# A right-hand side solved by two 64-row blocks instead of a last inversion level, 128-row operands for 8-row matmuls, and new turn strings

## The reference

```
S = S * exp(g_t)
u = (v_t - k_t . S) * b_t
S = S + outer(k_t, u)
o_t = q_t . S
```

## Time and profile before

| | before |
|---|---|
| median of three runs | 3089.29 us |
| the profiled execution | 3073.01 us |
| its span, first to last instruction | 3071.2 us |
| TensorE matmul busy | 2502.6 us (81%) |
| VectorE busy | 2245.6 us (73%) |
| ScalarE busy | 1247.8 us (41%) |
| GpSimd busy | 641.2 us (21%) |
| mean granted TensorE clock | 0.906 of full speed |

### The profile page before, as it was taken

How to read it: one execution, slowest core, us unless ns; L and a number is a source line. 1 busy time by engine, 2 the same in 40 slices (tenths; PEclk the granted TensorE clock), 3 DMA queues, 4 the chain that set the end, 5 groups by cost and what they waited for, 6 DMA issues and landing times.

```text
span 3071.2 us, 61542 instructions
## 1 busy us (share of the span) xinstructions
PE 2502.6 (81%) x22808; PEld 2004.1 (65%) x22808; DVE 2245.6 (73%) x5056; ACT 1247.8 (41%) x2761; POOL 641.2 (21%) x528
## 2 busy tenths in 40 slices
PE   2477978879887887978889797887988788897897
PEld 1166766757766576766757676575766657676686
DVE  1668777787877778787687877778787777877762
ACT  0233533435344253533425353243534424353342
POOL 0222122131212222122131212313121122202210
PEclk9869989989899898989989998998989989898998
DMA  4000000000000000000000000000000000000000
GB/s 119 2 2 3 2 8 3 7 3 7 2 3 8 2 7 3 6 2 3 7 3 7 2 3 8 3 7 3 7 2 3 7 3 7 3 4 5 1 5 2
DMA packets 24718, 21.52 MB, mean 7 GB/s; under 512 B 7210, under 2 KB 21443, under 8 KB 24403
## 3 DMA queue, kind: packets, MB, share of 16 engines
q1 hardware_dynamic: 24402, 17.14, 2.0%
HBM read 15.00 MB, written 2.13 MB: 6 GB/s over the span
## 4 chain that ended last, share of the span: by engine, by line
PE 60%; DVE 18%; issue 13%; POOL 4%; ACT 3%; SPq 1%; DMA 1%; DVEq 0%; POOLq 0%; ACTq 0%
PE banks L984 8%; PE banks L1160 8%; PE banks L1150 8%; PE banks L1034 6%; PE banks L918 4%; PE banks L927 3%; DVE wide L1332 3%; PE banks L976 3%; DVE wide L1344 2%; PE banks L855 2%; PE banks L962 2%; PE banks L1019 2%; PE banks L1026 2%; PE banks L897 2%; POOL lg L536 2%
## 5 line engine op out<-in xcount | busy, mean ns | idle before, releaser
L532 POOL TENSOR_TENSOR wide<-wide 128x512 f32<-128x512 f32 x128 | 243.5, 1902 | 872.5 <-DVE wide L1352 560.7
L1461 DVE SCALAR_TENSOR_TENSOR wide<-pad,conv,wide 128x256 f32<-128x256 f32 x864 | 389.1, 518 | 0.0
L984 PE MATMUL banks<-inv,mats 64*64 64x64 f32 x5120 | 198.0, 237 | 141.8 <-DVE inv L1505 104.6
L1344 DVE TENSOR_TENSOR_SCAN wide<-wide 128x1024 f32<-128x1024 f32 x128 | 308.4, 2409 | 1.9 <-ACT wide L634 0.3
L634 ACT ACTIVATE wide<-small,a_neg 128x255 f32<-128x255 f32 x512 | 217.8, 497 | 201.8 <-DVE wide L1344 198.9
L984 PEld LDWEIGHTS banks<-inv,mats 64*64 64x64 f32 x5120 | 185.2, 152 | 160.1 <-issue 159.2
L1150 PE MATMUL banks<-inv,up 128*128 128x256 f32 x1024 | 264.9, 387 | 0.0
L1160 PE MATMUL banks<-down,inv 128*128 128x128 f32 x2048 | 257.7, 277 | 0.0
L768 ACT ACTIVATE inv<-banks,up1b 128x256 f32<-128x256 f32 x512 | 215.0, 481 | 105.0 <-PE banks L1150 104.8
L1160 PEld LDWEIGHTS banks<-down,inv 128*128 128x128 f32 x2048 | 249.9, 192 | 5.8
L984 PE MATMUL banks<-inv 64*64 64x64 f32 x5120 | 189.0, 233 | 29.0 <-DVE inv L1513 28.9
(11 more groups left out here) (281 smaller groups left out, 5160.1 us busy)
## 6 DMA issues: line engine op xcount, KB each, us to landing
gates_bc<-gate_rows SPq DMA_DIRECT2D x32, 128.0 KB, 2.9
up<-in_W SPq DMA_DIRECT2D x1, 2048.0 KB
x<-in_x SPq DMA_DIRECT2D x16, 128.0 KB, 2.1
out<-xn_y SPq DMA_DIRECT2D x16, 128.0 KB, 1.9
wide<-in_wmod SPq DMA_DIRECT2D x2, 384.0 KB
con<-in_con SPq DMA_DIRECT2D x1, 724.0 KB
w_k<-in_Wk SPq DMA_DIRECT2D x1, 512.0 KB
w_q<-in_Wq SPq DMA_DIRECT2D x1, 512.0 KB
```

Source lines behind the costliest of these rows:

```text
L532: g.tensor_tensor(ypart[p % 2], r[:, 0:512], r[:, 512:1024], ALU.add).then_inc(a_yp.h, 1)
L984: last = t.matmul(PS[a:b, out, h * HALF:(h + 1) * HALF], weights(h, a, b), values(h, a, b), start=True, stop=True)
L1344: v.tensor_tensor_scan(state[st % 2], decay[st % 2], drive[st % 2], 0.0, ALU.mult, ALU.add).then_inc(a_h.h, 1)
L1461: v.scalar_tensor_tensor(dst, src, w, dst, ALU.mult, ALU.add).then_inc(c_conv.h, 1)
```

## The change

The last level is dropped: LEVELS ends at 32. What it made is replaced by a solve in two blocks per chunk. c_top multiplies the upper 64 rows of R by the inverse of the upper block, ScalarE copies the result to top_x; c_low multiplies it by the off-diagonal block of M, and VectorE adds that to the lower half of R; c_X multiplies this by the inverse of the lower block. All are 64x64 weights with 32 columns, 8 heads each. TTf is gone. keep_warm now stands ahead of c_top of chunk 1, and of c_low and c_X of both chunks.

cfT, rank_sb and w_dt get 128 rows, zero below the eighth or ninth, and the products L883 and L826 read all 128. The product with down0b in b_out still reads nine rows.

```diff
-LEVELS = [2, 4, 8, 16, 32, 64]
+LEVELS = [2, 4, 8, 16, 32]
...
-APPLY = [("c_R", 0), ("c_X", 0), ("c_U", 0), ("c_O", 0), ("c_S",), ("c_o", 0), ("c_kS",), ("c_R", 1), ("c_X", 1),
+APPLY = [("c_R", 0), ("c_top", 0), ("c_low", 0), ("c_X", 0), ("c_U", 0), ("c_O", 0), ("c_S",), ("c_o", 0), ("c_kS",), ("c_R", 1), ("c_top", 1), ("c_low", 1), ("c_X", 1),
...
-        "yyyyyyyyyxyxyyyyyyxyyxyyyyyyyyyyyxyyyyxxyyyxxyxxyxxyxxyxxyyxxxxxxxxyyxxyyxxyxxxxyxxyyyyxyxxyxyyx"
-        "yxyyyyyyyyyyyxyyxyyxyyxyyxyyxyyxyyyyyxxxxxxxxxxxxxxxxx"),
+        "yyyyxxyyyyyyyxyxyyyxyyxxyxyxyyyxxyyxxyxxyxyxyyyxxxxxxxxyyxxyyyxxxxxxyxxyyyyxyxyxyyyyxyxxyyyyyyyy"
+        "xyyxyxyxyyxyyyyyxxyyxxyxxxxxxxxyyxxxxxxyyx"),
-        "yyyyyyxyxyyyxyyxyxyyxyxyyyyxyyyyxxxyyxyxxyxxxyxxxyxyxxyxyxxxxxyxxxyyxxyxxyxxyxxyxxxxyxyyxyxxxyxy"
-        "xyxxyxxyxxyxyxyyxxxxxxxxx"),
+        "yyyxyyyyxyxyyyxyyxyyxxyyyxyxxxyxyyyxxyxyxxxyxxyxyxyxyxxxyxxxyxxxyyxxyxyxxxyxxyxxxxyxyyxyxxxxyxyy"
+        "xxxxxyxxyxxxxxxyxyxxyxy"),
-        "yyyyyxyyxyyyyxxyyyyxyxyyyxyyyxyxyyxxxyxxxyxxyyxxyxxxxyyxyyyxxxyxyyyyxyyxyxyxyxyxyxyxyyxxxxxxxxxx"),
+        "yxyxyyxyyxxyxxyyxxyyyxxxyyxyxxxxyyxxxyxxyxyxyyyxxxyyxyxyyyxyxyxxyxyxyyxyxxxxxyyxxxxx"),
-        "xxxxxxxxxyxyxxyxxxxxxxxxxxx"),
+        "xxxxxxxxyxxxyxyxxxxxxxxxxxx"),
...
-        w_dt = sb("w_dt", [RANK, CB * P])
+        w_dt = sb("w_dt", [P, CB * P])
...
-        rank_sb = sb("rank_sb", [RANK, T])
+        rank_sb = sb("rank_sb", [P, T])
...
-        cfT = sb("cfT", [9, T])
+        cfT = sb("cfT", [P, T])
...
-        TTf = sb("TTf", [P, TILES, NH, P])
+        top_x = inv[0:HALF, 6, 256:512].rearrange("p (h v) -> p h v", v=DV)
...
-            g.memset(TTf[:], 0.0)
+            g.memset(cfT[:], 0.0)
+            g.memset(rank_sb[:], 0.0)
...
-            def lev_T(i, l, ch):
-
-                if l + 1 == NL:
-                    s.wait_ge(c_Tp.h, c_Tp.at(i, ch + 1))
-                    s.copy(TN[ch][0:HALF].rearrange("p h t -> p (h t)"), PS[0:HALF, 5 + ch, :]).then_inc(c_Tl.h, 1)
-
             def lev_TT(i, l, ch):
-                if l + 2 < NL:
+                if l + 1 < NL:
                     s.wait_ge(c_T.h, c_T.at(i, (l + 1) * TILES + ch + 1))
                 else:
                     s.wait_ge(c_TTp.h, c_TTp.at(i, l * TILES + ch + 1))
-                if l + 2 < NL:
-                    last = s.copy(TTd[ch].rearrange("p h t -> p (h t)"), bank(5 + ch))
-                elif l + 2 == NL:
-                    for a, b in HALVES:
-                        last = s.copy(TTf[a:b, ch, :, a:b], PS[a:b, 5 + ch, :].rearrange("p (h t) -> p h t", t=HALF))
-                else:
-                    last = s.copy(TTf[0:HALF, ch, :, HALF:P], PS[0:HALF, 5 + ch, :].rearrange("p (h t) -> p h t", t=HALF))
-                last.then_inc(c_TT.h, 1)
+                s.copy(TTd[ch].rearrange("p h t -> p (h t)"), bank(5 + ch)).then_inc(c_TT.h, 1)
+
+            def c_top(i, ch):
+                s.wait_ge(c_tp.h, c_tp.at(i, ch + 1))
+                s.copy(top_x.rearrange("p h v -> p (h v)"), PS[0:HALF, 3 + ch, 0:256]).then_inc(c_tx.h, 1)
...
-                    t.matmul(bank(1, T), con[0:E0, C_SEL + m * P:C_SEL + (m + 1) * P], cfT[0:E0, :], start=True,
+                    t.matmul(bank(1, T), con[:, C_SEL + m * P:C_SEL + (m + 1) * P], cfT[:], start=True,
...
-            def lev_T(i, l, ch):
-                if l + 1 == NL:
-                    t.wait_ge(c_TT.h, c_TT.at(i, (l - 1) * TILES + ch + 1))
-                    t.sem_inc(released, 1)
-                    for h in range(NH):
-                        last = t.matmul(PS[0:HALF, 5 + ch, h * HALF:(h + 1) * HALF], TTf[0:HALF, ch, h, 0:HALF], ident[0:HALF, 0:HALF],
-                                        start=True, stop=True)
-                    last.then_inc(c_Tp.h, 1)
-
             def lev_Z(i, l, ch):
-                if l + 1 < NL:
-                    t.wait_ge(c_T.h, c_T.at(i, l * TILES + ch + 1))
-                else:
-                    t.wait_ge(c_Tl.h, c_Tl.at(i, ch + 1))
+                t.wait_ge(c_T.h, c_T.at(i, l * TILES + ch + 1))
                 t.sem_inc(released, 1)
-                if l + 1 < NL:
-                    last = halves(3 + ch, lambda h, a, b: MTc[ch][a:b, h, a:b], lambda h, a, b: TN[ch][a:b, h, :])
-                else:
-                    for h in range(NH):
-                        last = t.matmul(PS[HALF:P, 3 + ch, h * HALF:(h + 1) * HALF], MTc[ch][0:HALF, h, HALF:P], TN[ch][0:HALF, h, :],
-                                        start=True, stop=True)
-                last.then_inc(c_Z.h, 1)
+                halves(3 + ch, lambda h, a, b: MTc[ch][a:b, h, a:b], lambda h, a, b: TN[ch][a:b, h, :]).then_inc(c_Z.h, 1)
 
             def lev_TT(i, l, ch):
                 t.wait_ge(c_W.h, c_W.at(i, l * TILES + ch + 1))
                 if l >= 1:
                     t.wait_ge(c_TT.h, c_TT.at(i, (l - 1) * TILES + ch + 1))
                 t.sem_inc(released, 1)
-                if l + 2 < NL or l + 2 == NL:
-                    last = halves(5 + ch, lambda h, a, b: WW[ch][a:b, h, :], lambda h, a, b: TTd[ch][a:b, h, :])
-                else:
-                    for h in range(NH):
-                        last = t.matmul(PS[0:HALF, 5 + ch, h * HALF:(h + 1) * HALF], WW[ch][HALF:P, h, :], TTf[HALF:P, ch, h, HALF:P],
-                                        start=True, stop=True)
-                last.then_inc(c_TTp.h, 1)
+                halves(5 + ch, lambda h, a, b: WW[ch][a:b, h, :], lambda h, a, b: TTd[ch][a:b, h, :]).then_inc(c_TTp.h, 1)
...
-            def c_X_(i, ch):
+            def c_top(i, ch):
                 if ch == 1:
                     keep_warm(4)
                 if ch == 0:
                     t.wait_ge(c_R0.h, c_R0.at(i, 1))
-                    t.wait_ge(c_TT.h, c_TT.at(i, NL * TILES))
+                    t.wait_ge(c_TT.h, c_TT.at(i, (NL - 1) * TILES + 1))
                 else:
                     t.wait_ge(c_R1.h, c_R1.at(i, 3))
-                per_head(3 + ch, lambda h: TTf[:, ch, h, :], R).then_inc(c_X.h, 1)
+                    t.wait_ge(c_TT.h, c_TT.at(i, NL * TILES))
+                t.sem_inc(released, 1)
+                for h in range(NH):
+                    last = t.matmul(PS[0:HALF, 3 + ch, h * DV:(h + 1) * DV], TTd[ch][0:HALF, h, :], R[0:HALF, h, :], start=True, stop=True)
+                last.then_inc(c_tp.h, 1)
+
+            def c_low_(i, ch):
+                keep_warm(7 - ch)
+                t.wait_ge(c_tx.h, c_tx.at(i, ch + 1))
+                t.sem_inc(released, 1)
+                for h in range(NH):
+                    last = t.matmul(PS[HALF:P, 3 + ch, 256 + h * DV:256 + (h + 1) * DV], MTc[ch][0:HALF, h, HALF:P], top_x[:, h, :],
+                                    start=True, stop=True)
+                last.then_inc(c_lp.h, 1)
+
+            def c_X_(i, ch):
+                keep_warm(7 - ch)
+                t.wait_ge(c_low.h, c_low.at(i, ch + 1))
+                t.sem_inc(released, 1)
+                for h in range(NH):
+                    last = t.matmul(PS[HALF:P, 3 + ch, h * DV:(h + 1) * DV], TTd[ch][HALF:P, h, :], R[HALF:P, h, :], start=True, stop=True)
+                last.then_inc(c_X.h, 1)
...
-                elif l + 1 < NL:
+                else:
                     v.wait_ge(c_TTp.h, c_TTp.at(i, (l - 1) * TILES + ch + 1))
                     v.transpose(TN[ch].rearrange("p h t -> p (h t)"), bank(5 + ch)).then_inc(c_T.h, 1)
 
             def lev_Z(i, l, ch):
                 v.wait_ge(c_Z.h, c_Z.at(i, l * TILES + ch + 1))
-                if l + 1 < NL:
-                    v.tensor_tensor(WW[ch], bank(3 + ch).rearrange("p (h t) -> p h t", t=HALF),
-                                    con[:, C_MERGE + l * HALF:C_MERGE + (l + 1) * HALF].unsqueeze(1).broadcast_to([P, NH, HALF]),
-                                    ALU.mult).then_inc(c_W.h, 1)
-                else:
-                    v.tensor_copy(WW[ch][HALF:P].rearrange("p h t -> p (h t)"), PS[HALF:P, 3 + ch, :]).then_inc(c_W.h, 1)
+                v.tensor_tensor(WW[ch], bank(3 + ch).rearrange("p (h t) -> p h t", t=HALF),
+                                con[:, C_MERGE + l * HALF:C_MERGE + (l + 1) * HALF].unsqueeze(1).broadcast_to([P, NH, HALF]),
+                                ALU.mult).then_inc(c_W.h, 1)
...
+
+            def c_low_(i, ch):
+                v.wait_ge(c_lp.h, c_lp.at(i, ch + 1))
+                if ch == 0:
+                    v.wait_ge(c_R0.h, c_R0.at(i, 1))
+                else:
+                    v.wait_ge(c_R1.h, c_R1.at(i, 3))
+                v.tensor_tensor(R[HALF:P], R[HALF:P], PS[HALF:P, 3 + ch, 256:512].rearrange("p (h v) -> p h v", v=DV),
+                                ALU.add).then_inc(c_low.h, 1)
```

22 lines of the change are left out of this document (12 added, 10 removed).

## The result

The changed kernel takes 3093.51 us (median of 20 runs, 3088.31 to 3098.63) and the kernel before 3083.76 us (20 runs, 3077.88 to 3091.03), ratio 1.0029, 95% interval 1.0021 to 1.0036: 10 us slower, where I forecast 8 us faster. The profiled executions have spans of 3086.5 and 3071.2 us, 15.3 apart.

What follows compares the result with a forecast made beforehand. No engine bounds the whole: latency limits the first stage, VectorE the scan, TensorE the projections. Terms sum to -0.35 us an iteration, times 15 -5, and -2.7 once: -8 us, 3081 us, range 3040 to 3122.

Steps and rivals of the forecast that it cites:

- the turn of the loop: End of each iteration: d_res, VectorE's last step, lies bare before the issue gap, +0.9 us; upper bound 1.4.
- The clock: TensorE at half clock: half of 1.2 us lost in the solve, a third of 1.0 won in the first stage, +0.3.
- rival B: In the new solve, VectorE waits for c_low at a low TensorE clock; +25 us, 3114 us; chance 0.25.
- The new solve: Last level: VectorE swaps copies for additions (-0.55 us) and waits less (-0.46), together -1.0 an iteration; last half -2.7 once.
- The start of the scan: Scan stage: the new order of a_soft, a_step and a_scan(0) starts the scan 3.1 us earlier; bounds 1.0 and 4.5.
- Inside the full stage: Scan stage, where VectorE is full: lev_T(4,1) and two merges move in, +1.9 us; the last level's change wins 1.0.
- POOL's order: End of the scan: c_squares ahead of step 6's sum puts one more sum in line, +1.35 us; upper bound 1.8.
- The middle: Chain after the scan: with d_scores ahead of b_coef, b_out starts 0.4 us earlier; bounds -1.0 and +0.6.
- The projection stage: Expert and projection matmuls: reordered TensorE work fills gaps before the value transposes, -0.3 us; bounds -0.4 and +3.
- rival D: Projection stage: the new order starves TensorE; at 2 us an iteration +22 us, 3111 us; chance 0.06.
- 128 rows: Coefficient products priced at 0.59 to 0.69 us, four times an iteration; 128-row a_dt could spare up to 1.0 on average.
- The signs: First scan some 34 us in, VectorE over 95% busy in the scan, addition's wait under 0.5 us, or over 1 for rival B.

Runs made afterwards that it cites:

- dres_last: tail_early with only d_res moved to the end of VectorE's order; ratio 1.0027 to the kernel before.
- dres_fills: four_fills with d_res last and 12 pairs of unread matmuls at the turn of the loop; ratio 0.9848 to the kernel before.
- dt128_only: The kernel before with 128 rows for w_dt and rank_sb alone; ratio 1.0004 to the kernel before.
- rows8_after: The changed kernel with 8 (and 9) rows again for w_dt, rank_sb and cfT; ratio 1.0051 to the kernel before.
- fill_solve: The changed kernel with unread matmuls in TensorE's idle time between the level-4 products; ratio 1.0031 to the kernel before.
- solve_only: The kernel before with the new solve alone, 8 rows and old order; ratio 0.9962 to the kernel before.
- squares_late: The changed kernel with POOL's old order, c_squares between the pair sums of steps 6 and 7; ratio 1.0025 to the kernel before.
- coef128_only: The kernel before with 128 rows for cfT and the coefficient products alone; ratio 0.9935 to the kernel before.
- tail_early: The changed kernel with the old TensorE, VectorE and ScalarE order from the ninth projection step on; ratio 0.9899 to the kernel before.
- fill_turn: The changed kernel with 14 pairs of unread matmuls in TensorE's idle time at the turn of the loop; ratio 0.9949 to the kernel before.
- tail_early_fill_turn: tail_early with 14 pairs of unread matmuls at the turn of the loop; ratio 0.9965 to the kernel before.
- three_fills: tail_early with fill_solve's unread matmuls and 9 pairs at the turn of the loop; ratio 1.0021 to the kernel before.
- four_fills: three_fills with unread matmuls also at the last two scan steps, a_out and d_turn; ratio 0.9783 to the kernel before, 3013.6 us.

## Why the prediction was wrong

**The step that failed** is the turn of the loop: "It lies bare before that gap: 2 x 0.46 = +0.9. Upper bound 1.4". By dres_last it costs 2.6 us an iteration, 40 us in all. About half is bare time: TensorE's idle time grows by 1.4 us, the edge of my upper bound (dres_fills: 21 us). The other half is that a longer idle time brings the clock back later, in level 0 (2.84 us for 2.21) and behind it. I priced the added idle time as time alone, and had the rows to see more: the earlier trace rows showed the clock at 0.67 there and the two kinds of iteration in the earlier trace rows were worth 2 us. With 0.9 changed to 2.6, my sum of -0.35 becomes +1.35 us an iteration, 15 times, less 2.7: +18, as against +10 in the runs and +15 in the profiled pair. That it comes so near is partly luck: the start of the scan and the full stage were off by 1 us or more each, and the -6.5 of the x half alone was in no term.

**The clock** was the second. I priced it per stage, half of 1.2 in the solve and a third of 1.0 in the first stage. In the first stage the 3.52 us group is gone from the iterations, more than the third that I took. But a_dt's rows, my reason, bring nothing (dt128_only, 1.0004), and rows8_after has level 3 at the low clock with iterations of the same length: as time the term was worth nothing there. The solve's 1.2 came as a wait of 1.77 us at the place that rival B named, in every iteration, within its 1.2 to 4.1. But B's price was no price of the time: fill_solve took the wait away and nothing was won. The clock in one stage and the next are not independent terms; what the solve gained stayed only with all four idle stretches filled.

**The new solve**: right in sign, two thirds of the size. -1.0 us an iteration and -2.7 in the last half make 18; solve_only measured 0.38%, 12 us. The last half is 2.4 shorter.

**The start of the scan**: 2.05 us earlier for my 3.1, in an iteration of the kind that I walked, and 3.0 against the mean of both kinds. The walk put a_step 1.6 earlier; it is 0.4 (31.6 after c_first for 32.0), and level 0 has taken 0.9 of the missing 1.2: its products take 3.68 and 2.84 us behind the longer turn, for 3.37 and 2.20.

**Inside the full stage** I had +1.9 moved in and -1.0 won. From the first drive to VectorE's last step ahead of c_squares it is +3.1. The rest is waits: 1.77 at c_low(0), 0.45 at the level-4 merge, 0.25, 0.28 and 0.26 elsewhere; and one scan of 3.36 us has become one of 2.29.

**POOL's order**: +1.35 forecast. The stretch from read 7 to a_res did grow, from 7.4 and 7.9 us by turns to 8.3, but not by the place of the squares: squares_late has the same 8.3, and solve_only, with POOL's old order, has 8.3 to 9.3. As far as these runs show, it goes with the new solve. The sum of step 6 was late in both orders.

**The middle**: -0.4 forecast, -0.5 (27.1 us from a_res to b_res for 27.6), right by luck. I had it from the order; rows8_after has the new order and takes 27.6, coef128_only has the old one and takes 27.2. It is the rows. **The projection stage**: -0.3 forecast, -0.1 (59.8 for 59.9), and rival D is out. The 0.1 us of the earlier trace rows, in which I saw the drain at a change of the tiling mode, is no sign of it: the 128-row coefficient pair takes 0.70 us too, between pairs of 0.59.

**128 rows**: priced at 0.59 to 0.69 a pair, with a clock gain for a_dt alone. The pair is 0.70 in the trace, dearer if anything, and the kernel before gains 0.7% by the coefficient products; in the x half alone that is the clock, in the iterations it isn't shown. In the changed kernel most of that is lost, since rows8_after is only 7 us slower.

Taken one by one, the change is -0.7% by the rows and -0.4% by the solve, with nothing to be seen of the new order up to the eighth projection step (tail_early -1.0%, the two alone -1.1%), and +1.3% by d_res. The parts don't simply add: with d_res last the rows are worth 0.2%.

**The signs** that I named: the first scan at 35.1 us for my 34; VectorE 93% busy in the scan stage for over 95; its wait 1.77 us, (B)'s side; the squares before two sums, the projection stage of 59.8 us and the two residual instructions as said. (B)'s sign came and wasn't the cause.

The Trainium skill (TensorE: Matmul & The Clock Gate, Part 1, What's actually happening) says that the throttled state is the default and activity releases it. The runs agree, fill_turn above all: matmuls with no use made the kernel 25 us faster. By that rule alone I would have given the longer turn a clock price. The Trainium skill (Perfetto Trace Analysis, Matmul Optimizations) also asks for matmuls back to back in batches; of this kernel's stages only the fourth has them so, and it alone had the clock at 1.00 before.

**What stays open.** Why the middle gives back what the solve gained (fill_solve), and what decides whether an iteration of the kernel before is of 181 or 184 us, isn't settled. What the 128-row products cost or gain besides the clock isn't either, nor is how they shorten the iterations of the kernel before, nor why VectorE's issue gap at the turn is 2.57 us in the changed kernel and 2.3 in dres_last, with d_res last in both.

## What to carry to other kernels

Idle time of TensorE on a latency chain cost twice here, once as time and once as the clock of what follows; so look at how long TensorE idles at the turn of a loop, and let nothing that could run earlier stand last there. One filled gap alone brought 0.8% (fill_turn), nothing (fill_solve) or harm (tail_early_fill_turn), while filling all of them brought 1.2 to 1.7% in three versions; see that each filler is shorter than its wait, by the start of the product behind it. When a kernel's iterations come in two lengths, price a change for both kinds, and take the mean.

## What was not expected of the hardware

- The rows of an operand told on the clock. In the x half alone TensorE stayed at 1.2 GHz for the whole of the routed experts with 8-row coefficient products (1.22 us a pair to the end), and with 128 rows it was at 2.4 after 5 us (0.60). coef128_only, which changes those products alone, shows it too (12 us for the stretch, 18 in every version with 8 rows), and is 0.65% faster than the kernel before.
- The issue gap at the turn of the loop isn't a constant of an engine. VectorE's was 2.0 us in the kernel before and tail_early, 2.3 in dres_last and 2.6 in the changed kernel. TensorE's own was 2.1, and with 18 fillers behind it a second stop of 2.47 us came in three_fills and none in four_fills, which differ only elsewhere in the program.
- With fillers that nobody reads, the mean iteration went from 180.9 us (tail_early) to 178.6 (four_fills).
